# Where the rank product and the steps behind it stand among the shared expert's items

## The chip, the cores and the metric

One core of one Trainium2 chip. The time is the device time of one execution in microseconds; the median of three executions of the kernel before is 1052.46 us (1050.67 to 1053.14).

## What is computed

A residual stream `x` of 2 x 1024 tokens and 256 features passes four blocks, each behind a layer norm: attention with one key head, a feed-forward block, attention with ALiBi, and the same feed-forward block again. The change lies in the two feed-forward blocks:

```
shared_out = silu(x @ sw1.T) * (x @ sw2.T) @ sw3.T          # hidden 1024
scores = sigmoid(x @ router_w.T)                            # 8 experts
top_idx = top_k(scores + expert_bias, 2)
combine = the two scores, divided by their sum, at the two experts
h = silu(h1) * h2        # h1, h2 = x @ w12 of the expert, 128 wide
routed_out = sum over experts of (h @ w3) * combine
x = x + shared_out + routed_out
```

## The kernel before, in words

All engines run hand-written queues that meet at semaphores. Products that need fp32 accuracy are made of three passes over a high and a low part of each operand (lines 246 to 248 for an up product, line 1196 for a down product).

**Items.** The shared expert is cut into eight units of 128 hidden features and the tokens into four chunks of 512; `ITEMS` (line 45) orders the 32 pairs. Per item `e`, TensorE makes the up product `up(f, e)` (12 matmuls of 512 columns into banks 2(e mod 2) and 2(e mod 2)+1), ScalarE the gate `sg`, VectorE the product `hf` (`hidden`, L1893), ScalarE its high part `hh` (L1430), VectorE the low part `hl` (L1897), and TensorE the down product `down(f, e)`. TensorE's order is up(e), down(e-1), up(e+1), ... VectorE can't do anything between `hf` and `hl` of one item, since its queue is in order. Items 0 to 3 go before the loop that matters here (in `between`), items 4 to 15 in `feed_forward` ahead of the routed experts, 16 to 31 behind them. f is 0 or 1 for the two feed-forward blocks.

**Routing.** The tokens of each expert must be gathered into tiles before the routed products can start. That takes a long series of small VectorE steps, placed behind `hidden` of an item by two tables, `ROUTE_BEHIND` and `FIND_BEHIND` (item: stages), and by two TensorE products placed behind the up product of an item:

- `route` stages 0 to 2 (L1803 to L1819): the best two experts of each token, as a 0/1 table `chosen`.
- `count_ranks`, behind up(RANK_AT) (L1207, L1208): four matmuls over `chosen`, into `rank_bank`, which is the gate bank of the other parity than RANK_AT. It waits for `chosen` and for `hf` of the item before.
- `route` stage 3 (L1823, L1824): copies the ranks and counts out of that bank. It is called by item RANK_AT - 1, as the last of that item's work, and waits for the rank product. The up product of item RANK_AT + 1 waits for these copies.
- `route` stages 4 to 6 (L1827 to L1857): prefix sums and each token's place `pos`.
- `find` stages 0 to 6 (L1907 to L1928): from `pos` the tables `is_tile` (stage 1), four quarters of `in_tile` (stages 2, 3, 5, 6; L1921), `at_tile` (stage 4).
- `find_sources`, behind up(FIND_AT), FIND_AT = 13 (L1215): 32 matmuls over them. It waits for all of find 0 to 6.
- `find` stage 7 (L1933 to L1938), behind item 13: `source_f`, `source`. The up product of item 14 waits for `source_f` (L1935).
- POOL then issues the indirect DMAs that gather the rows (`fetch_rows`, L842), and TensorE turns them (`turn_rows`, L1231) ahead of and behind down(15).
- `route` stages 7 to 9: the two weights of each token and the experts' places, behind items 13 to 15.

**Weight splits.** Behind each odd item from 5 to 13 ScalarE casts (L1498) and VectorE subtracts (L1944) the weights of a further unit; `EXPERT_BEHIND` places the same two steps (L1504, L1950) for experts 6 and 7, and POOL splits the other six.

VectorE's order within an item (lines 1952 to 1964):

```
hidden(f, e)
for stage in FIND_BEHIND.get(e, ()):
    find(f, stage)
for stage in ROUTE_BEHIND.get(e, ()):
    route(f, stage)
if e in EXPERT_BEHIND:
    expert_low(f, EXPERT_BEHIND[e])
if e % 2 and RING <= (e + 3) // 2 < 2 * SHARED and e != 2 * SHARED - 1:
    unit_low(f, (e + 3) // 2)
if e == RANK_AT - 1:
    route(f, 3)
```

Of the kernel before, what the change touches and what calls it, by code (L numbers as in the profile page):

```python
# [44 lines left out]
ITEMS = [(u, 0) for u in range(3)] + [(u, 1) for u in range(3)] + [(u, c) for u in range(3, SHARED) for c in (0, 1)] + \  # L45
        [(u, c) for u in range(SHARED) for c in (2, 3)]
OPENING = 3
RANK_AT, FIND_AT = 6, 13
ROUTE_BEHIND = {3: (0,), 4: (1,), 5: (2,), 6: (4, 5), 7: (6,), 13: (7,), 14: (8,), 15: (9,)}
FIND_BEHIND = {8: (0, 1, 2), 9: (3,), 10: (4,), 11: (5,), 12: (6,), 13: (7,)}  # L50
FIND = 10
UNIT_IN_ROUTED = 4
EXPERT_BEHIND = {12: 6, 14: 7}
COMBINE_BEHIND = [{18: 3, 19: 3, 20: 3, 21: 1, 22: 3, 23: 3, 24: 1, 25: 1, 26: 1, 27: 3, 28: 3, 29: 3, 30: 3, 31: 1},
                  {**{e: 3 for e in range(18, 28)}, 28: 2}]
STATS_BEHIND = {21: 0, 24: 1}
# [195 lines left out]
def program(nc, x, w_a, b_a, fc_a, b_fc, w_b, fc_b, w_units, router, ebias, iota, consts, slopes, krows, out):  # L252
# [15 lines left out]
    with ExitStack() as ctx:  # L268
# [1052 lines left out]
        def _(act):  # L1321
# [104 lines left out]
            def high(f, e):  # L1426
                s = FS * f + e
                act.wait_ge(h_done, s + 1)
                wait(act, down_done, s - 1)
                act.copy(hh[:, e % 2, :], hf[:, e % 2, :]).then_inc(hh_done, 1)  # L1430
# [69 lines left out]
            def expert_high(f, e):  # L1500

                cols = slice(WIDTH * e, WIDTH * e + WIDTH)
                act.wait_ge(wexp_in[e], 16 * (f + 1))
                act.copy(wexp_h[:, cols], wexp_raw[:, cols]).then_inc(exp_high_done, 1)  # L1504

            def unit_item(f, e):

                gate(f, e)
                high(f, e)
                if e in EXPERT_BEHIND:  # L1510
                    expert_high(f, EXPERT_BEHIND[e])
                if e % 2 and RING <= (e + 3) // 2 < 2 * SHARED and e != 2 * SHARED - 1:
# [27 lines left out]
        def _(dve):  # L1540
# [345 lines left out]
            def hidden(f, e):  # L1886

                s = FS * f + e
                a = e % 2
                dve.wait_ge(silu_done, s + 1)  # L1890
                dve.wait_ge(u_ready, s + 1)
                wait(dve, hl_done, s - 1)
                dve.tensor_tensor(hf[:, a, :], bank[2 * a + 1], sg[:, a, :], ALU.mult).then_inc(h_done, 1)  # L1893
                if f == 0 and e in TURNED:
                    lows(2, TURNED[e])
                dve.wait_ge(hh_done, s + 1)
                dve.tensor_tensor(hl[:, a, :], hf[:, a, :], hh[:, a, :].bitcast(F32), ALU.subtract).then_inc(hl_done, 1)  # L1897
# [48 lines left out]
            def expert_low(f, e):  # L1946

                cols = slice(WIDTH * e, WIDTH * e + WIDTH)
                dve.wait_ge(exp_high_done, (NEXP - POOL_EXPERTS) * f + e - POOL_EXPERTS + 1)
                dve.tensor_tensor(wexp_l[:, cols], wexp_raw[:, cols], wexp_h[:, cols].bitcast(F32), ALU.subtract).then_inc(exp_low_done, 1)  # L1950

            def unit_item(f, e):
# [9 lines that stand above are left out]
# [177 lines left out]
```

## Time and profile before

| | |
|---|---|
| median of 3 executions | 1052.46 us (1050.67 to 1053.14) |
| the profiled execution's own time | 1053.91 us |
| its span, first to last instruction | 1052.2 us |
| mean granted TensorE clock | 0.988 |
| VectorE busy | 758.8 us (72%) |
| ScalarE busy | 589.2 us (56%) |
| GpSimd busy | 409.8 us (39%) |
| chain that ended last | PE 78%, DVE 13%, ACT 4%, issue 3%, POOL 2%, DMA 1% |

Engines: PE is TensorE's matmuls, PEld its weight loads, DVE VectorE, ACT ScalarE, POOL GpSimd, SP SyncE. Times in the timeline count from the start of the span. A row of the timeline is an instruction or a run of like ones: its start, how long it takes, engine, line, operation, what it writes and reads, and, in brackets, how long the engine had stood idle and who released it. Ends of matmuls are modelled, so the time that a product takes is best read from start to start. Items 4 to 15 of the first feed-forward block run from 346.69 to 401.12 us; in the second block they begin 518.79 us later.

### The profile page before, as it was taken

How to read it: one execution, taken by the hardware profiler on the slowest of the kernel's cores; microseconds unless marked ns; L12 is line 12 of the kernel's file. 1: busy time of each engine (PE TensorE's matmuls, PEld its weight loads, DVE VectorE, ACT ScalarE, POOL GpSimd, SP SyncE). 2: the span in 40 equal slices, each digit the busy share in tenths (PEclk: the TensorE clock that was granted, in tenths of full speed). 3: DMA queues.
4: the chain of work that ended last, by engine and by line, in shares of the span. 5: the costliest groups of instructions: out<-in, count | busy, mean ns of one | idle time of the engine just before them, and what ended most of it. 6: DMA issues, size and time to landing. Idle time of an engine off the chain costs nothing.

```text
span 1052.2 us, 19787 instructions
## 1 busy us (share of the span) xinstructions
PE 997.4 (95%) x6818; PEld 639.3 (61%) x6818; DVE 758.8 (72%) x1564; ACT 589.2 (56%) x1262; POOL 409.8 (39%) x434
## 2 busy tenths in 40 slices
PE   4789999999999999999989999999999999999998
PEld 3533433343348889988867433333443588899887
DVE  6788888888447686447778878888883658764575
ACT  4525776777764335653445657777777543466432
POOL 3420544322443507625743102322234362274470
PEclk9969999999999999999999999999999999999999
DMA  4721121110114315734249523244401151256351
GB/s 133 193 41 32 44 42 43 40 42 13 30 26 154 137 45 160 187 111 120 77 116 224 104 43 58 54 75 74 76 10 46 31 211 61 71 178 167 119 180 51
DMA packets 66756, 95.23 MB, mean 91 GB/s; under 512 B 19670, under 2 KB 50822, under 8 KB 64600
## 3 DMA queue, kind: packets, MB, share of 16 engines
q1 hardware_dynamic: 46645, 52.54, 18.3%
q10 hardware_dynamic: 13100, 22.53, 8.8%
q0 software_dynamic: 6912, 18.88, 7.0%
q8 instruction: 57, 0.93, 0.4%
q14 instruction: 42, 0.34, 0.1%
HBM read 66.59 MB, written 26.67 MB: 89 GB/s over the span
## 4 chain that ended last, share of the span: by engine, by line
PE 78%; DVE 13%; ACT 4%; issue 3%; POOL 2%; DMA 1%; ACTq 0%; SPq 0%; DVEq 0%; POOLq 0%
PE o_ps L1056 14%; PE st_ps L1038 11%; PE su_ps L997 8%; PE st_ps L246 7%; PE st_ps L247 7%; PE st_ps L248 7%; DVE mab L1678 5%; PE st_ps L997 4%; PE o_ps L1196 4%; PE su_ps L1196 3%; PE su_ps L1102 3%; ACT pt L1404 2%; PE st_ps L1231 2%; PE su_ps L1001 2%; PE su_ps L246 1%
## 5 line engine op out<-in xcount | busy, mean ns | idle before, releaser
L1404 ACT ACTIVATE pt<-st_ps 128x512 f32<-128x512 f32 (+3 forms) x768 | 329.0, 494 | 175.1 <-PE st_ps L1038 118.1
L1038 PE MATMUL st_ps<-qs,ks 99*128 99x512 bf16 (+9 forms) x768 | 245.2, 333 | 9.1 <-ACT pt L1404 6.2
L761 POOL TENSOR_SCALAR_AFFINE_SELECT pt<-pt 128x512 f32<-128x512 f32 x120 | 76.4, 637 | 352.0 <-ACT pt L1404 352.0
L1678 DVE TENSOR_REDUCE mab<-su_ps 128x1 f32<-128x512 f32 (+3 forms) x302 | 190.0, 659 | 22.9 <-PE su_ps L1001 16.4
L1056 PE MATMUL o_ps<-pt,vp 128*32 128x512 f32 (+3 forms) x1536 | 164.5, 503 | 1.9 <-POOL pt L761 1.0
L997 PE MATMUL su_ps<-ks,qs 102*128 102x512 bf16 (+7 forms) x538 | 160.8, 328 | 4.7 <-DVE mc L1678 2.7
L1038 PEld LDWEIGHTS st_ps<-qs,ks 99*128 99x128 bf16 (+2 forms) x768 | 73.7, 98 | 115.9 <-ACT pt L1404 64.4
L842 POOL DMA_INDIRECT rows_in<-rows,source x80 | 78.5, 981 | 98.0 <-DVE source L1938 73.7
L1678 DVE TENSOR_REDUCE mab<-st_ps 128x1 f32<-128x512 f32 (+2 forms) x152 | 100.2, 660 | 13.7 <-PE st_ps L1001 10.4
L1430 ACT CAST hh<-hf 128x512 fp32r<-128x512 f32 x64 | 39.7, 621 | 123.8 <-DVE hf L1893 123.8
L997 PEld LDWEIGHTS su_ps<-ks,qs 96*128 96x128 bf16 (+1 forms) x538 | 52.6, 98 | 83.1 <-DVE mab L1678 48.5
L246 PE MATMUL st_ps<-xt_h,wu 128*128 128x512 f32 x256 | 100.9, 394 | 1.4 <-DVE source_f L1935 0.9
L247 PE MATMUL st_ps<-xt_h,wu 128*128 128x512 f32 x256 | 100.3, 392 | 0.0
L248 PE MATMUL st_ps<-xt_l,wu 128*128 128x512 f32 x256 | 99.7, 389 | 0.0
L852 POOL DMA_INDIRECT back<-outs,pos x64 | 68.1, 1064 | 61.3 <-DMA outs<-rows_out 39.8
L997 PE MATMUL st_ps<-ks,qs 96*128 96x512 bf16 (+6 forms) x230 | 78.9, 356 | 4.9 <-DVE mc L1678 2.0
L1897 DVE TENSOR_TENSOR hl<-hf,hh 128x512 fp32r<-128x512 f32 x64 | 44.6, 696 | 42.6 <-ACT hh L1430 42.6
L1678 DVE TENSOR_REDUCE mc<-su_ps 128x1 f32<-128x512 f32 (+3 forms) x105 | 63.2, 620 | 15.7 <-PE su_ps L1001 15.7
L1001 PE MATMUL su_ps<-cstb 128*128 128x128 bf16 x370 | 70.9, 222 | 0.0
L1893 DVE TENSOR_TENSOR hf<-st_ps,sg 128x512 f32<-128x512 f32 x64 | 43.9, 686 | 29.1 <-PE st_ps L248 23.6
L1056 PEld LDWEIGHTS o_ps<-pt,vp 128*32 128x32 f32 x1536 | 31.1, 109 | 51.2 <-issue 35.9
L1423 ACT ACTIVATE sg<-st_ps 128x512 f32<-128x512 f32 x64 | 38.2, 597 | 42.8 <-PE st_ps L248 42.6
(230 smaller groups left out, 2033.3 us busy)
## 6 DMA issues: line engine op xcount, KB each, us to landing
wu_raw<-w_units_dram SPq DMA_DIRECT2D x32, 384.0 KB, 3.1
outs<-rows_out ACTq DMA_DIRECT2D x40, 256.0 KB, 2.8
q_parts<-hml SPq DMA_DIRECT2D x16, 384.0 KB, 3.3
wexp_raw<-w_units_dram SPq DMA_DIRECT2D x16, 384.0 KB, 7.1
inv<-inverses SPq DMA_DIRECT2D x128, 32.0 KB, 1.8
rows<-xn SPq DMA_DIRECT2D x8, 512.0 KB, 6.9
qs<-q_parts ACTq DMA_DIRECT2D x10, 384.0 KB
k_parts<-hml SPq DMA_DIRECT2D x8, 384.0 KB, 2.6
```

Source lines behind the costliest of these rows:

```text
L246: pe.matmul(out, lh, rh, start=n == 0, stop=False)
L247: pe.matmul(out, ll, rh, start=False, stop=False)
L248: last = pe.matmul(out, lh, rl, start=False, stop=n == len(terms) - 1)
L761: pool.affine_select(block, block, [[0, 4], [1, P]], ALU.is_ge, 0.0, base=0, channel_multiplier=-1).then_inc(masked, 1)
L842: pool.indirect_dma_start(rows_in[:, n % RPAIRS, a, :], None, rows, bass.IndirectOffsetOnAxis(ap=source[:, 2 * i + a:2 * i + a + 1], axis= ...
L997: last = pe.matmul(out_b[:, c0:c0 + width], query_columns(s, slice(0, rows), j0 + a, P * qt, P * qt + P), key_stack(l, s)(j0 + a)[0:rows, ...
L1001: last = pe.matmul(out_b[:, c0 + width - P:c0 + width], identb, mask_q, start=False, stop=True)
L1038: last = pe.matmul(bank[KM_BANKS[n % len(KM_BANKS)]][:, lo - CH * part:hi - CH * part], key_stack(l, s)(j)[0:rows, P * kt:P * kt + P], que ...
L1056: last = pe.matmul(o_ps[32 * j:32 * j + 32, lo:hi], vp[:, QT * b + kt, 4 * g + j if l else 4 * (g % 2), :], exponentials(s, q, lo, hi)[:, ...
L1196: last = pe.matmul(out_b, left, right, start=u == 0 and n == 0 and t % 2 == 0, stop=u == SHARED - 1 and n == 2, skip_group_check=True)
L1404: act.activation(exponentials(s, q, lo, hi)[:, j, :], bank[KM_BANKS[i % len(KM_BANKS)]][:, lo - CH * part:hi - CH * part], ACT.Exp, scale= ...
L1678: dve.tensor_reduce(to, bank[SU_BANKS[n % len(SU_BANKS)]][:, 0:share * width].rearrange("p (j k) -> p j k", j=share), AX.X, ALU.max).then_ ...
```

## The change

`RANK_AT` goes from 6 to 7, so the rank product goes behind item 7's up product, and the copies of its results behind item 6's `hidden` instead of item 5's. Route stages 4, 5 and 6 go behind items 7 and 8 (before: 6 and 7), find stages 0 to 6 behind items 9 to 12 (before: 8 to 12), and the split of expert 6 behind item 11 (before: 12), on ScalarE and VectorE. `rank_bank` changes with RANK_AT from bank 2 to bank 0.

```diff
-RANK_AT, FIND_AT = 6, 13
-ROUTE_BEHIND = {3: (0,), 4: (1,), 5: (2,), 6: (4, 5), 7: (6,), 13: (7,), 14: (8,), 15: (9,)}
-FIND_BEHIND = {8: (0, 1, 2), 9: (3,), 10: (4,), 11: (5,), 12: (6,), 13: (7,)}
+RANK_AT, FIND_AT = 7, 13
+ROUTE_BEHIND = {3: (0,), 4: (1,), 5: (2,), 7: (4,), 8: (5, 6), 13: (7,), 14: (8,), 15: (9,)}
+FIND_BEHIND = {9: (0, 1), 10: (2, 4), 11: (3,), 12: (5, 6), 13: (7,)}
 FIND = 10
 UNIT_IN_ROUTED = 4
-EXPERT_BEHIND = {12: 6, 14: 7}
+EXPERT_BEHIND = {11: 6, 14: 7}
```

## Rows read from the trace of the kernel before

**Rows 1.** The page, part 1: busy time of TensorE, weight loads and the others.

```profile
PE 997.4 (95%) x6818; PEld 639.3 (61%) x6818; DVE 758.8 (72%) x1564; ACT 589.2 (56%) x1262; POOL 409.8 (39%) x434
```

**Rows 2.** The waits of PE, 344 to 400 us: total, times, longest.

```profile
PE st_ps L1207 <- DVE chosen L1819: 0.7, 1, 0.7
PE st_ps L246 <- DVE source_f L1935: 0.5, 1, 0.5
PE su_ps L1196 <- DVE hl L1897: 0.3, 1, 0.3
```

**Rows 3.** The timeline of DVE, items 5 to 13 of the first feed-forward block.

```profile
357.57 0.69 DVE L1897 TENSOR_TENSOR hl<-hf,hh 128x512 fp32r<-128x512 f32 x1 [0.69 <-ACT hh L1430]
...
360.10 0.29 DVE L1823 COPY rank<-st_ps 128x128 f32<-128x128 f32 x1
...
360.50 0.68 DVE L1893 TENSOR_TENSOR hf<-st_ps,sg 128x512 f32<-128x512 f32 x1
...
362.48 0.42 DVE L1827 TENSOR_TENSOR_SCAN cum<-cst,filled 128x128 f32<-128x128 f32 x1
...
363.51 0.28 DVE L1837 TENSOR_REDUCE few<-over 128x8 f32<-128x128 f32 x1
...
388.10 1.22 DVE L1921 TENSOR_TENSOR in_tile<-steps_in,pos_partf 128x1024 bf16<-128x1024 f32 x1
389.24 0.95 DVE L1950 TENSOR_TENSOR wexp_l<-wexp_raw,wexp_h 128x768 fp32r<-128x768 f32 x1
390.11 0.68 DVE L1893 TENSOR_TENSOR hf<-st_ps,sg 128x512 f32<-128x512 f32 x1
...
392.31 0.20 DVE L1935 SCALAR_TENSOR_TENSOR source_f<-st_ps,source_f 128x40 f32<-128x40 f32 x1
392.55 0.18 DVE L1938 CAST source<-source_f 128x40 uint32<-128x40 f32 x1
```

**Rows 4.** The timeline of PE: first rows of products, items 5 to 14.

```profile
355.69 0.40 PE L246 MATMUL st_ps<-xt_h,wu 128*128 128x512 f32 x1
...
359.35 0.49 PE L1207 MATMUL st_ps<-chosen,cst 128*128 128x128 f32 x2 [0.75 <-DVE chosen L1819]
359.67 0.39 PE L1208 MATMUL st_ps<-chosen,cst 128*128 128x128 f32 x2
359.81 0.36 PE L1196 MATMUL su_ps<-wu,hh 128*128 128x256 f32 x1
...
361.33 0.40 PE L246 MATMUL st_ps<-xt_h,wu 128*128 128x512 f32 x1
...
364.08 0.28 PE L1196 MATMUL o_ps<-wu,hh 128*128 128x256 f32 x1
...
365.51 0.40 PE L246 MATMUL st_ps<-xt_h,wu 128*128 128x512 f32 x1
...
389.38 1.32 PE L1215 MATMUL st_ps<-at_tile,in_tile 128*128 128x80 bf16 x32
390.53 0.36 PE L1196 MATMUL o_ps<-wu,hh 128*128 128x256 f32 x1
...
392.66 0.47 PE L246 MATMUL st_ps<-xt_h,wu 128*128 128x512 f32 x1 [0.46 <-DVE source_f L1935]
```

**Rows 5.** The timeline of POOL: the first gather of the first block.

```profile
393.62 1.98 POOL L842 DMA_INDIRECT rows_in<-rows,source  x1 [36.91 <-DVE source L1938]
```

**Rows 6.** The timeline of ACT: expert 6's cast.

```profile
387.37 0.83 ACT L1504 CAST wexp_h<-wexp_raw 128x768 fp32r<-128x768 f32 x1
```

**Rows 7.** The timeline of PE: the second turn of gathered rows, first block.

```profile
403.06 0.66 PE L1231 MATMUL st_ps<-cst,rows_in 128*128 128x128 f32 x4 [1.34 <-DMA rows_in<-rows,source]
```

**Rows 8.** The timeline of PE: the first two turns of the second block.

```profile
919.90 1.03 PE L1231 MATMUL st_ps<-cst,rows_in 128*128 128x128 f32 x8
```

**Rows 9.** Windows: busy time of PE, PEld, DVE, ACT, POOL, granted clock, DMA share.

```profile
50.00:55.00 5.00, 3.62 (x15) 1.32 (x15) 4.90 (x11) 0.00 (x0) 0.00 (x0) 0.64 0.64 120
55.00:60.00 5.00, 4.73 (x17) 2.22 (x17) 4.09 (x8) 2.25 (x4) 0.00 (x0) 0.50 0.92 177
...
540.00:545.00 5.00, 3.15 (x14) 2.25 (x13) 5.00 (x11) 2.31 (x6) 2.87 (x3) 1.00 0.68 236
```

## The prediction

> **What bounds the kernel now.** I read the page first: TensorE (PE) is busy 95% of the span [rows 1], so a change of order can win only PE's waits, and can lose whatever new wait it makes. So the second view was PE's waits in the stretch that the change touches, items 3 to 15 of the first feed-forward layer. There are three, 1.5 us together [rows 2]: the rank product waits 0.7 us for `chosen`, item 14's up product 0.5 us for `source_f`, one down product 0.3 us for `hl`. The second layer repeats the first 518.79 us later, wait for wait.
>
> The third view was VectorE's (DVE) timeline [rows 3]. The reader is to see that every `hf` starts the moment the work in front of it ends: from 357.57 to 392.55 DVE waits for nothing but its own round trip through ScalarE (ACT) between `hf` and `hl`. Such a `hidden` costs DVE 1.98 us from `hf` to the next instruction (360.50 to 362.48) [rows 3]. The seven items 6 to 12 take it from 360.50 to 390.11, 4.23 us each. PE needs 2.75 us for an up product (361.33 to 364.08) and 1.43 for a down product (364.08 to 365.51) [rows 4], 4.18 per item. So PE is nominally the bound, but in this stretch DVE is as full as PE and runs behind it; it decides when `find_sources` can start: 389.38, 0.06 us behind the end of the last `in_tile` (388.10 + 1.22) [rows 3, 4].
>
> **The change part by part.** No instruction is added or removed; per layer the same work is reordered, and only the placing behind items differs. The queues of SP and POOL are as before: POOL's gathers wait for `source` alone [rows 5].
>
> Ranks behind item 7's up product. Removed: PE's wait. Item 6's up product starts at 355.69 and would end at 358.44; the rank product started at 359.35 [rows 4], so 0.91 us is gained here. `hl` of item 5 ends at 357.57 + 0.69 = 358.26 [rows 3], so item 5's down product can follow at 358.44. PE then: down 5 to 359.87, up 7 to 362.62, rank product there. Its results were out at 359.67 + 0.39 = 360.06, 0.71 behind its start, and PE was free for the next after 0.46 (359.35 to 359.81) [rows 4]. I take the same: results at 363.35, `rank` copied from 363.40.
>
> Where the wait goes: DVE. Now the copy of the ranks comes directly behind `hidden` of item 6 and the next instruction on DVE is queued behind it. Before, item 4's unit split (DVE L1944) filled the wait, and the copy started at 360.10 with no idle. After, `hf` of item 6 can start at 360.1 at the latest (360.50 less the 0.40 of the two copies) [rows 3], its `hidden` ends at 362.1, and DVE stands until 363.40. This is a wait that no row of before shows. Bounds: nothing, if the product were out when `hidden` ends; at most 2.75, a whole up product. I take 1.3, worked out above from rows on both sides.
>
> The stages behind items 7 to 12. The copies end at 363.80. What DVE did before from 362.48 (first instruction behind `hidden` 6) to 388.10 (the last `in_tile`) is 25.62 us, with no wait in it that another order would save. The new order has the same work there, and one thing more: expert 6's split now comes ahead of the last `in_tile` instead of behind it, 0.87 us (389.24 to 390.11) [rows 3]. So the last `in_tile` starts at 363.80 + 25.62 + 0.87 = 390.29 and ends at 391.51; `find_sources` starts at 391.57, **2.19 us later than before**. PE would be ready for it at about 388.7 (from 362.62: 0.46 for the ranks, six pairs of a down and an up product of 4.18 = 25.1, and 0.5 for a wait of item 11's down product for its `hl`, which DVE's lag by then makes), so it stands for 2.9 us in one piece. Cover check: DVE must not run out of input in between. `hf` of item 7 starts at 363.80, 1.0 us behind its product. Item 7 costs 1.98 + 1.03 (route stage 4, 362.48 to 363.51) + 0.87, so `hf` of item 8 starts at 367.68; its up product ends near 367.4. That margin of 0.3 is the thinnest. Items 8 to 11 then take (387.2 - 367.7) / 4 = 4.88 us each against PE's 4.18, so DVE only falls further behind.
>
> Bank of the ranks: item 8's up product now waits for the copies, at 363.9; it would start at 364.5. Nothing. Expert 6 on ACT: the 0.83 us cast [rows 6] now goes in front of item 12's gate, which is needed on DVE at 387.2; even with the unit cast of the same item it is done 1.4 us earlier. Nothing; without that cover at most 0.83.
>
> Behind find. Item 12's down product follows 1.15 us after `find_sources` starts (389.38 to 390.53), item 14's up product at 391.57 + 1.15 + 1.43 = 394.15, against 392.66 [rows 4]: 1.49 later, and the 0.5 us wait for `source_f` is gone (ready at 392.51 + 1.32 = 393.8). About 0.1 comes off, because that product no longer restarts a standing array. DVE: `hf` of item 13 moves from 390.11 to 391.43, 1.32 later, and with it `source`, POOL's first gather (393.62) [rows 5] and the landing. In the first layer PE waits 1.34 us for the gathered rows, to 403.06 [rows 7]: the landing decides, +1.32. In the second both first turns run together at 919.90 without a wait [rows 8]: PE decides, +1.4. The landings themselves are bounded: they may slip by less than 1.34 in the first layer where they meet other transfers; I take no slip. From there on PE, DVE and POOL are shifted alike, so nothing is given back.
>
> **Sum.** 1.32 + 1.4 = +2.7 us, of which the price of the rank wait is 1.3 per layer, expert 6's place 0.87 for find, less 0.9 that PE gained ahead and cannot spend. The profiled execution took 1053.91 us around a span of 1052.2, so 1056.6 for such a one; it stands 1.45 above the median of 1052.46, so the median becomes 1055.2.
>
> One term can be weighed against a rule. The rows show 0.46 us for the rank product with the array standing before it [rows 4]; that is what the sum uses. The Trainium skill (TensorE: Matmul & The Clock Gate, Architectural detail: the array is 16× 32×32, not 1× 128×128) says that TensorE can pull weight loads ahead of running matmuls; now that `chosen` is ready long before, the load would be hidden, an estimate of 0.1 us less per layer and +2.5 in place of +2.7. The wait row cannot show it.
>
> **The rivals.** About 0.2% (2.1 us) is what a measurement of this kernel can tell from no change.
> (a) My forecast, 0.67: 1055.2, between 1.5 and 3.8 us above before.
> (b) The ranks come while `hidden` 6 still runs, so DVE does not stand. Then only the 0.87 us of expert 6 delays find, and DVE reaches `source` when it did: 1052.5. For it: PE is 1.46 us ahead at item 7 (359.87 for 361.33). Against: the product must be out before 362.1, and item 7's up product alone ends at 362.62. 0.15, mostly for a DVE stretch that has slack I don't see.
> (c) Faster: PE's order decides to the end of the stage. The wait for `chosen` goes (0.91), and find waits no longer than before: 1.0 us per layer, 1050.5. It decides if the last `in_tile` ends before 388.2 (362.62 + 0.46 + 25.1), so DVE would have to be 3.3 us quicker over items 6 to 12 than I work out. Nothing shows that. 0.08.
> (d) TensorE's clock falls in the new 2.9 us hole. The rows show a granted clock of 0.64 and then 0.50 (half speed, 1.2 GHz) over 50 to 60 us, behind a sparsely used PE; that stretch lost 5 x 0.36 + 5 x 0.50 = 4.3 us of full speed. Against it, 540 to 545 stands idle for 1.85 of 5 us and keeps 1.00 [rows 9]. Once in one layer: 1055.2 + 4.3 = 1059.5. 0.10. The Trainium skill (the same page, What's actually happening) has TensorE at half rate after it stood idle for long enough and at full rate after sustained work; by it the length of the hole decides, and the trace agrees in so far as the hole of 540 to 545 cost nothing, while no row of this case has one of 2.9 us between dense products.
>
> **How the numbers follow.** The predicted time is (a)'s. The range 1051.4 to 1058.2 leaves out (c) and (d), and takes in (b) and the bounds of the rank wait and the landings for (a). Of (a)'s 0.67 some 0.13 lies under the 0.2% bound. Faster 0.08; same 0.15 + 0.13 = 0.28; slower 0.54 + 0.10 = 0.64.
>
> **What the changed profile would show.** Right: no wait of PE for `chosen`; DVE idle 1.3 us before `rank`, released by PE; item 11's down product waiting some 0.5 us for `hl`; PE idle nearly 3 us before L1215, released by `in_tile`; no wait for `source_f`; `source` 1.3 us later in both layers, and the turns of gathered rows as much. Wrong: a `rank` copy with no idle before it (b), a find wait under 0.5 us (c), or a granted clock under 1.00 within 390 to 400 us (d). If DVE has idle time before `hf` of item 8, the thin margin was no margin and the loss is larger.

## The result, and the profile after

| | before | changed |
|---|---|---|
| median of 7 executions | 1053.47 us | 1058.99 us |
| lowest and highest | 1050.67, 1054.10 | 1054.54, 1061.12 |
| profiled execution, own time and span | 1053.91, 1052.2 | 1054.54, 1052.8 |
| mean granted TensorE clock | 0.988 | 0.990 |

The ratio is 1.0046, 95% interval 1.0031 to 1.0061: the change makes the kernel slower by 4.8 us (3.3 to 6.4; the two medians lie 5.5 apart). I had forecast slower by 2.7 and a range up to 1058.2, so the direction was right and the size too small; the median of 1058.99 lies 0.8 above the range. One microsecond of that distance is no fault of the change's account: the median before is 1053.47 over seven executions, and I had started from 1052.46, that of three.

The profiled execution is the fastest of the seven and ends only 0.6 us behind that of before. So spans don't compare the two; places inside the stage do. The copy of the scores (L1784) opens it, and the time from there to a later instruction of the stage, up to the first turn of gathered rows, repeats mostly to 0.01 to 0.05 us between traces of one kernel, where the clock does not fall (0.10 in e11 and e15). Behind that turn it does not: it scatters by microseconds. Up to that copy the changed kernel's execution was 2.98 us ahead (343.81 for 346.79), by chance of the first attention: in fifteen further traces, whose code is the same up to there, the copy lies anywhere between 344.09 and 350.14. Behind it the changed kernel loses 2.17 us by the second block's copy and 1.41 in the second block: 0.6 = -2.98 + 2.17 + 1.41.

The waits of PE in the changed kernel, 344 to 402 us (total, times, longest), against [rows 2]:

```profile
PE st_ps L1215 <- DVE in_tile L1921: 2.7, 1, 2.7
PE su_ps L1196 <- DVE hl L1897: 0.6, 2, 0.3
```

The waits for `chosen` and `source_f` are gone; one wait of the find product stands in their place, nearly twice as long as the three of before together. The timeline of DVE, to be read against [rows 3]:

```profile
357.03 0.68 DVE L1893 TENSOR_TENSOR hf<-st_ps,sg 128x512 f32<-128x512 f32 x1
...
360.29 0.29 DVE L1823 COPY rank<-st_ps 128x128 f32<-128x128 f32 x1 [1.20 <-PE st_ps L1208]
...
386.16 2.35 DVE L1921 TENSOR_TENSOR in_tile<-steps_in,pos_partf 128x1024 bf16<-128x1024 f32 x2
388.43 0.68 DVE L1893 TENSOR_TENSOR hf<-st_ps,sg 128x512 f32<-128x512 f32 x1
...
390.86 0.18 DVE L1938 CAST source<-source_f 128x40 uint32<-128x40 f32 x1
```

DVE stands 1.20 us for the ranks, where it stood for nothing before. The timeline of PE in the first block, against [rows 4]:

```profile
359.65 0.38 PE L1207 MATMUL st_ps<-chosen,cst 128*128 128x128 f32 x2
...
388.56 1.37 PE L1215 MATMUL st_ps<-at_tile,in_tile 128*128 128x80 bf16 x32 [2.68 <-DVE in_tile L1921]
389.74 0.56 PE L1196 MATMUL o_ps<-wu,hh 128*128 128x256 f32 x1
...
392.44 0.63 PE L246 MATMUL st_ps<-xt_h,wu 128*128 128x512 f32 x1
```

Item 12's down product takes 2.70 us from start to start (389.74 to 392.44) where a down product takes 1.43. The windows say why; the column before the last two is the granted clock:

```profile
388.00:389.00 1.00, 0.43 (x12) 0.44 (x13) 1.00 (x2) 0.00 (x0) 0.00 (x0) 1.00 0.00 0
389.00:390.00 1.00, 1.00 (x26) 1.00 (x23) 0.32 (x2) 0.86 (x2) 0.00 (x0) 0.85 0.00 0
390.00:391.00 1.00, 1.00 (x6) 1.00 (x7) 0.93 (x5) 0.49 (x1) 0.00 (x0) 0.50 0.00 0
...
392.00:393.00 1.00, 1.00 (x6) 0.90 (x5) 0.82 (x1) 0.00 (x0) 1.00 (x1) 0.50 0.00 0
393.00:394.00 1.00, 1.00 (x6) 0.83 (x5) 0.00 (x0) 0.00 (x0) 0.92 (x1) 0.95 0.00 0
```

Some 1.1 us after the hole's end the clock falls, and TensorE works at half clock (1.2 GHz) for some 3 us. The second block has the same hole and no such stretch; its up product of item 14 follows the find product by 2.65 us, where the first block's took 3.88:

```profile
909.53 1.32 PE L1215 MATMUL st_ps<-at_tile,in_tile 128*128 128x80 bf16 x32 [2.68 <-DVE in_tile L1921]
...
912.18 0.40 PE L246 MATMUL st_ps<-xt_h,wu 128*128 128x512 f32 x1
```

### The profile page after: what moved, and what is told of

Read it like the earlier page. It is cut to its first block, busy times and chain, and to the rows that moved or that the text cites. A ratio compares the mean times of both kernels' runs of the same rounds, so it can differ in the third digit from the quotient of the medians.

```text
span 1052.8 us, 19785 instructions
## 1 busy us (share of the span) xinstructions
PE 994.1 (94%) x6818; PEld 637.6 (61%) x6818; DVE 758.9 (72%) x1564; ACT 588.7 (56%) x1262; POOL 411.3 (39%) x434
## 4 chain that ended last, share of the span: by engine, by line
PE 76%; DVE 14%; ACT 4%; issue 3%; POOL 2%; DMA 1%; ACTq 0%; SPq 0%; DVEq 0%; POOLq 0%
PE o_ps L1056 14%; PE st_ps L1038 11%; PE su_ps L997 7%; PE st_ps L246 7%; PE st_ps L247 7%; PE st_ps L248 7%; DVE mab L1678 5%; PE o_ps L1196 4%; PE su_ps L1196 4%; PE st_ps L997 4%; PE su_ps L1102 2%; ACT pt L1404 2%; PE st_ps L1231 2%; PE su_ps L1001 2%; PE su_ps L246 1%
## 5 line engine op out<-in xcount | busy, mean ns | idle before, releaser
L246 PE MATMUL st_ps<-xt_h,wu 128*128 128x512 f32 x256 | 100.9, 394 | 0.4 <-DVE xt_l L1570 0.4
```

Of the source, the lines that this page charges most:

```text
L246: pe.matmul(out, lh, rh, start=n == 0, stop=False)
```

## The experiments

All comparisons inside the stage are in one measure: microseconds from the copy of the scores, less the same in the kernel before, first block / second block. Positive is later; the values are good to 0.02 us.

| kernel | find product starts | `source` | up product of item 14 | first turn of gathered rows |
|---|---|---|---|---|
| forecast for the change | 2.19 | 1.32 | 1.49 | - |
| changed kernel | 2.16 / 2.17 | 1.29 / 1.29 | 2.76 / 1.54 | 2.97 / 1.46 |
| e1, the same | 2.17 / 2.16 | 1.81 / 1.29 | 3.70 / 3.08 | 4.27 / 3.00 |
| e9, the same | 2.20 / 2.20 | 1.86 / 1.34 | 3.02 / 1.59 | 2.93 / 1.51 |
| e2, hole filled | 2.18 / 2.16 | 1.30 / 1.29 | 1.56 / 1.54 | 1.47 / 1.45 |
| e3, unit 4 in the rank wait | 2.15 / 2.17 | 1.79 / 1.30 | 2.92 / 1.56 | 2.82 / 1.47 |
| e5, expert 6 behind find | 1.30 / 1.29 | 1.30 / 1.28 | 1.30 / 1.28 | 1.28 / 1.27 |
| e6, before with expert 6 behind 11 | 1.09 / 0.86 | 0.22 / -0.01 | 0.47 / 0.25 | 0.37 / 0.16 |
| e7, expert 6 in the rank wait | 1.29 / 1.31 | 0.42 / 0.43 | 0.68 / 0.69 | 0.58 / 0.60 |
| e8, splits on GpSimd | 4.29 / 4.54 | 3.42 / 3.66 | 3.67 / 3.93 | 3.57 / 3.83 |
| e11, before with late splits | -0.23 / -0.24 | -0.69 / -0.70 | -0.70 / -0.71 | -0.69 / -0.70 |
| e12, and scores from PSUM | -1.42 / -1.41 | -1.88 / -1.87 | -1.89 / -1.88 | -1.90 / -1.86 |

The experiments ran in five groups. In that of e5 to e8 the kernel before takes 1054.67 us, like in the result; in the other four it takes 1087.7 to 1092.9 us, and single executions of it lie up to 15 us apart. I call these the slower groups; what makes them slower was not found. It need not be the chip: e5 to e8 and the slower e13 to e16 are on record under the same chip number. The table's measure is the same in both kinds: before's own second trace (e4) agrees with its first to 0.01 us in every column. The whole times of the slower groups are weak evidence.

**The changed kernel again (e1), and with TensorE kept at work in the hole (e2).** My theory of the surplus: the hole lets the clock fall. The rival: it comes from the opening.

> The changed kernel once more, for a second trace. Clock theory (the new hole of 2.7 us in front of the find matmuls lets the granted clock fall to 0.50 behind it in some executions, in one block or both): find_sources starts 2.2 us and item 13's hf 1.3 us later than before relative to the start of the stage, in both blocks; the stretch behind the hole is at 0.50 for some 3 us in one or both blocks, and the time is 3 to 7 us above before. Rival (the surplus over my 2.7 us arises elsewhere, in the first attention's opening, whose clock is low in stretches): the holes look as in the first trace, and the span up to the copy of the scores (L1784) is longer than the 346.8 us of before by the surplus.

> The changed kernel with 15 idle bf16 matmuls of 384 columns (results unused) in front of the wait of find_sources, so that TensorE works through the hole while VectorE's order and every start of the find matmuls stay. Clock theory: no stretch under 1.00 behind the find matmuls, and the time falls by 1.5 to 3.5 us against the changed kernel, to 2 to 3.5 us above before. Rival (elsewhere): the time stays within 1 us of the changed kernel, about 5 us above before.

```diff
 def find_sources(f):
-    pe.wait_ge(find_step, FIND * f + FIND - 1)
     pe.wait_ge(h_done, FS * f + FIND_AT)
+    for _ in range(15):
+        pe.matmul(found_bank[:, P:4 * P], identb, cstb[:, :, :].rearrange("p a m -> p (a m)"), start=True, stop=True)
+    pe.wait_ge(find_step, FIND * f + FIND - 1)
```

e1: in both blocks the clock fell, item 14 came 3.70 and 3.08 us late. The windows of 8 us behind each find product of e1:

```profile
390.40:398.40 8.00, 8.00 (x55) 7.36 (x56) 3.56 (x10) 1.95 (x3) 3.50 (x3) 0.61 0.08 22
931.74:939.74 8.00, 8.00 (x65) 7.49 (x66) 4.17 (x11) 2.01 (x4) 3.83 (x4) 0.79 0.15 44
```

And of e2, where the find product starts at the same place of the stage (0.22 us of hole left, the rest filled):

```profile
394.91 1.32 PE L1217 MATMUL st_ps<-at_tile,in_tile 128*128 128x80 bf16 x32 [0.22 <-DVE in_tile L1923]
```

```profile
394.91:402.91 8.00, 8.00 (x73) 7.30 (x74) 5.11 (x13) 3.31 (x5) 3.87 (x3) 1.00 0.12 35
935.08:943.08 8.00, 8.00 (x73) 7.29 (x74) 5.12 (x13) 3.31 (x5) 3.84 (x4) 1.00 0.17 49
```

VectorE's lateness is untouched (find 2.18 later, source 1.30), and item 14 comes 1.56 and 1.54 later, what I had forecast (1.49). One pair could be chance, since the clock doesn't fall behind every hole; with the three more pairs below (no fall behind 8 filled holes, 7 behind 12 unfilled ones) it is shown inside the stage that the idle array is what lets the clock fall. The whole times don't show it: e1 1.0016 (0.9997 to 1.0036), e2 1.0026 (1.0010 to 1.0042).

**e4, the kernel before again.**

> The kernel before once more, for a second trace of it. Both theories: every wait of the feed-forward stage as in the first trace (0.7, 0.5 and 0.3 us). The rival expects the stretch up to the copy of the scores to differ from 346.8 us by some us, as it does between the two first traces (343.8 in the changed kernel's).

Its copy of the scores lies at 346.33; every column of the table is as in the first trace. It is the reference trace for the slower groups.

**Unit 4's split in the wait for the ranks (e3).**

> The changed kernel with unit 4's low part (L1944, 0.87 us) moved from behind item 5 to behind item 6, ahead of the copies of the ranks, so that it lies in VectorE's wait for the ranks. My theory (VectorE's queue decides when find starts): the wait in front of the rank copy falls from 1.2 to about 0.3 us, find starts 0.9 us earlier, the hole falls from 2.7 to 1.8 us, and the time falls by 1.7 us, and by the clock's share as well (together 2 to 4). Rival (TensorE's order decides, VectorE's wait is free): time unchanged within 0.5 us.

```diff
-if e % 2 and RING <= (e + 3) // 2 < ...:
+if e % 2 and e != 5 and RING <= (e + 3) // 2 < ...:
     unit_low(f, (e + 3) // 2)
+if e == 6:
+    unit_low(f, 4)
 if e == RANK_AT - 1:
     route(f, 3)
```

A miss, and a useful one. The wait stayed as it was:

```profile
361.13 0.95 DVE L1944 TENSOR_TENSOR wu<-wu_raw,wu 128x768 fp32r<-128x768 f32 x1
363.28 0.29 DVE L1823 COPY rank<-st_ps 128x128 f32<-128x128 f32 x1 [1.20 <-PE st_ps L1208]
```

Item 6's `hf` comes 0.88 us earlier for it and the split follows; the copy waits for a rank product whose time TensorE sets. Work that already lay ahead of the wait shortens nothing when it is moved into it. Only what lay behind it does, which is e7. Ratio 1.0023 (1.0008 to 1.0039).

**Which part of the change costs what (e5, e6, e7).** e5 takes expert 6 out of the way of find, e6 is the expert's move alone, e7 fills the rank wait with it.

> The changed kernel with the split of expert 6 back behind item 12, so behind the last in_tile; ranks and stages stay as changed. My theory (the find matmuls start when VectorE's queue, pinned by the end of the rank product, has done its work): in both blocks find starts 1.29 us later than before relative to the copy of the scores, in place of 2.16; source stays 1.29 later; item 14's up product now waits again for source_f and comes 1.3 later (1.54 in the changed kernel without a fall of the clock); the hole is 1.8 to 1.9 us. Clock theory: with a hole under 2 us the clock stays at 1.00. Time 2 to 3 us above before, below the changed kernel by 2. Rival (the place of expert 6 is free, only the ranks' place counts): find still 2.16 later.

> The kernel before with only the split of expert 6 moved from behind item 12 to behind item 11; ranks behind item 6 as before. My theory: find starts 0.87 us later than before, source not later, item 14's up product 0.1 to 0.2 later, hole in front of find 1.1 us, no fall of the clock: time within 0.5 us of before. Rival (expert 6's place is what costs): item 14's up product 0.9 us or more later in both blocks, 2 us in the time.

> The changed kernel with expert 6's split moved to behind item 6, into VectorE's wait for the ranks. Unlike unit 4's split, which lay in front of the wait already, this takes 0.87 us out of the work behind the ranks. My theory: the wait before the rank copy falls from 1.2 to 0.35 us, find 1.29 and source 0.42 us later than before (in place of 2.16 and 1.29), item 14's up product 0.5 to 0.6 later, no fall of the clock; time 1 us above before. Rival (VectorE's wait is not what delays source): source still 1.29 later.

```diff
# e5, from the changed kernel
-EXPERT_BEHIND = {11: 6, 14: 7}
+EXPERT_BEHIND = {12: 6, 14: 7}
# e6, from the kernel before
-EXPERT_BEHIND = {12: 6, 14: 7}
+EXPERT_BEHIND = {11: 6, 14: 7}
# e7, from the changed kernel
-EXPERT_BEHIND = {11: 6, 14: 7}
+EXPERT_BEHIND = {6: 6, 14: 7}
```

The waits of PE in e5 around find, from the timeline:

```profile
387.98 1.32 PE L1215 MATMUL st_ps<-at_tile,in_tile 128*128 128x80 bf16 x32 [1.82 <-DVE in_tile L1921]
...
391.26 0.47 PE L246 MATMUL st_ps<-xt_h,wu 128*128 128x512 f32 x1 [0.45 <-DVE source_f L1935]
```

Find came 1.30 later, 0.87 less than in the changed kernel, and item 14 waits for `source_f` again, 1.30 and 1.28 late: expected 1.29 and 1.3. Time 1.0028 (1.0010 to 1.0046), 2.9 us, as expected. So the ranks' place alone, with the stages behind it, costs 1.3 us per block and carries the larger part of the loss. e6: find 0.86 later in the second block, source on time, item 14 0.25 later (expected 0.1 to 0.2); in the first block item 4's `hf`, ahead of the edit, was already 0.21 late. Time 1.0008 (0.9993 to 1.0023). The expert's move alone costs little, because find was hidden from `source` by `hf` of item 13.

In e7 the wait for the ranks shrank from 1.20 to 0.22:

```profile
362.89 0.29 DVE L1823 COPY rank<-st_ps 128x128 f32<-128x128 f32 x1 [0.22 <-PE st_ps L1208]
```

Find 1.29 and 1.31 later, source 0.42 and 0.43 (expected 1.29 and 0.42), item 14 0.68 (expected 0.5 to 0.6). Time 0.9996 (0.9982 to 1.0010): 0.87 us of split work, put into the wait instead of behind it, takes 0.87 us off the lateness of item 14, and the whole time is again within the measurement of before (-1.9 to 1.1 us), although item 14 still comes 0.68 late. In e5 and e7 the hole before find is 1.8 us and the clock kept 1.00 in all four; four are too few to call such a hole safe, as a hole of 1.85 us elsewhere shows (the section on why the prediction was partly right).

**VectorE relieved by GpSimd (e8).** If VectorE's queue is the bound, taking four splits of 0.87 us (3.5 us) out of it ahead of find should make the changed order pay.

> The changed order, with VectorE relieved: experts 6 and 7 wholly, and the low parts of units 5, 6 and 7, on GpSimd, which stands idle from 356 to 393 us. My theory (VectorE's queue is the bound of this stretch, and the moved rank product pays only where it isn't): find starts 0.6 to 0.7 us earlier than before and item 14's up product 1.3 to 1.5 earlier in each block, source 1.5 earlier, no hole, no fall of the clock; time 2.5 to 3 us below before. Rival (GpSimd's work slows VectorE or comes late for the up products): new waits of PE for wu or slower instructions on VectorE, and no gain.

```diff
-POOL_EXPERTS = 6
+POOL_EXPERTS = 8
+POOL_UNITS = (5, 6, 7)
-EXPERT_BEHIND = {11: 6, 14: 7}
+EXPERT_BEHIND = {}
# ... behind split_expert on GpSimd; VectorE leaves these units out, and two waits are
# fitted to the new owner of the splits (not shown)
+for n in POOL_UNITS:
+    _, r = unit_turn(f, n)
+    pool.wait_ge(unit_high_done, LATE * f + n - RING + 1)
+    pool.wait_ge(unit_low_done, LATE * f + n - RING)
+    pool.tensor_tensor(wu[:, r, 1, :], wu_raw[:, r, 1, :], wu[:, r, 0, :].bitcast(F32), ALU.subtract).then_inc(unit_low_done, 1)
```

The rival won: 1.0068 (1.0047 to 1.0089), 7.2 us slower, item 14 3.67 and 3.93 later. VectorE's timeline of e8:

```profile
360.10 1.90 DVE L1824 TENSOR_TENSOR chosen<-eq,eq 128x128 f32<-128x128 f32 x1
...
367.68 1.58 DVE L1836 TENSOR_TENSOR over<-few,steps_in 128x128 f32<-128x128 f32 x1
```

and GpSimd's:

```profile
359.80 1.97 POOL L832 TENSOR_TENSOR wexp_l<-wexp_raw,wexp_h 128x768 fp32r<-128x768 f32 x1
367.23 1.89 POOL L869 TENSOR_TENSOR wu<-wu_raw,wu 128x768 fp32r<-128x768 f32 x1 [5.46 <-ACT wu L1503]
```

`chosen` took 0.37 us before and takes 1.90, ending at 362.00, 0.23 behind GpSimd's subtraction (361.77); `over` took 0.29 and takes 1.58, ending at 369.26 behind one that ends at 369.12. Two more instructions ahead of `chosen` suffer: the cast `idf` (L1819, at 357.15) takes 1.84 instead of 0.17, and the first `eq` (at 359.02) 0.84 instead of 0.29. An instruction that reads PSUM kept its length while GpSimd subtracted (`hf` at 355.18: 0.67, GpSimd's from 353.84 to 355.68). Item 6's `hf` came 3.24 us late, and the rank product stood 1.8 us for it. That GpSimd shares its SBUF interfaces with VectorE, and that VectorE instructions with two SBUF inputs contend for them, is what the Trainium skill states (GPSIMD Engine Reference, Specifications); the rows of `chosen` and `over` agree, and add the size: the small instruction lasts to just behind the end of the large one.

**Less work on VectorE ahead of `source` (e11, e12).** The same clash is in the kernel before, with nothing changed: the first instruction of route stage 0, and what GpSimd does then:

```profile
348.99 1.93 DVE L1803 TENSOR_TENSOR sel<-sc,ebb 128x128 f32<-128x128 f32 x1
```

```profile
348.60 2.17 POOL L831 TENSOR_TENSOR wexp_l<-wexp_raw,wexp_h 128x768 fp32r<-128x768 f32 x1
```

> The kernel before (ranks behind item 6) with VectorE's work ahead of source cut by 0.87 us and ahead of find by 0.87 as well: the split of expert 6 behind item 13, where VectorE has idle time, the low part of unit 7 behind item 12. My theory: find 0.2 us earlier (TensorE's order is then the bound), source 0.87 earlier, item 14's up product 0.8 to 0.9 earlier in each block; time 1.6 us below before. Rival (source_f is not what holds item 14): 0.2 earlier and no more.

> The same, and the addition of the expert bias to the scores reads them from PSUM, before their copy, instead of from SBUF. In the kernel before that instruction (L1803, 128x128) takes 1.93 us where like ones take 0.29; with more splits on GpSimd three further VectorE instructions with two SBUF inputs took 0.84 to 1.90 us, each to the end of GpSimd's subtraction. Theory (such a VectorE instruction stands while GpSimd runs one with two SBUF inputs): the addition takes 0.3 us, VectorE is 1.6 us ahead from item 4 on, PE waits neither for hl of item 3 nor for chosen, find 1.4 to 1.7 us and item 14's up product 1.9 to 2.3 us earlier than before in each block (relative to the copy of the scores); time 4 us below before. Rival (the instruction is slow by itself, by its broadcast input): still 1.9 us, and the time as in the run without it.

```diff
# e11, from the kernel before
-EXPERT_BEHIND = {12: 6, 14: 7}
+EXPERT_BEHIND = {13: 6, 14: 7}
-if e % 2 and RING <= (e + 3) // 2 < ...:
+if e % 2 and e != 11 and RING <= (e + 3) // 2 < ...:
     unit_low(f, (e + 3) // 2)
+if e == 12:
+    unit_low(f, 7)
# e12 adds, in between(), ahead of the copy of the scores (a wait for the bias moves with it)
+dve.tensor_tensor(sel[:, :, :], bank[6][:, 0:TT * NEXP].rearrange("p (t e) -> p t e", e=NEXP),
+                  ebb[:, :].unsqueeze(1).to_broadcast([P, TT, NEXP]), ALU.add).then_inc(rt_step, 1)
# and in route, stage 0
-dve.tensor_tensor(sel[:, :, :], sc[:, :, :], each(ebb[:, :]), ALU.add).then_inc(rt_step, 1)
```

e11: find 0.23 earlier (expected 0.2), item 14 0.70 (expected 0.8 to 0.9). e12: the addition takes 0.29 us when it reads PSUM:

```profile
348.70 0.29 DVE L1786 TENSOR_TENSOR sel<-su_ps,ebb 128x128 f32<-128x128 f32 x1 [5.81 <-PE su_ps L1120]
...
357.70 1.49 DVE L1899 TENSOR_TENSOR hl<-hf,hh 128x512 fp32r<-128x512 f32 x1 [0.69 <-ACT hh L1430]
```

```profile
347.84 1.82 POOL L831 TENSOR_TENSOR wexp_l<-wexp_raw,wexp_h 128x768 fp32r<-128x768 f32 x1
...
356.79 1.85 POOL L831 TENSOR_TENSOR wexp_l<-wexp_raw,wexp_h 128x768 fp32r<-128x768 f32 x1
```

It does so while GpSimd subtracts (347.84 to 349.66), and with the same broadcast input, so the rival that the instruction is slow by itself is refuted.

VectorE is 2.0 us ahead at item 5, find 1.42 and item 14 1.89 us earlier in both blocks (expected 1.4 to 1.7 and 1.9 to 2.3); `chosen` is still waited for, 0.3 us in place of 0.7. The lead of 2.0 us shrinks to 1.2 there, because the clash comes back in another place: item 5's `hl` (357.70) meets GpSimd's next subtraction and takes 1.49 us, where it took 0.69; e16 and the second blocks show the same. In the whole time e11 has 0.9983 (0.9964 to 1.0002) and e12 0.9989 (0.9970 to 1.0008). Both ran again:

> The kernel before with expert 6's split behind item 13 and unit 7's low part behind item 12, again: item 14's up product 0.70 earlier in each block as in its first trace, time 1.2 to 1.8 us below before.

> The same with the scores' addition reading PSUM, again: item 14's up product 1.9 earlier in each block as in its first trace; time 3 to 4 us below before where nothing behind the stage gives it back.

e15: 0.9987 (0.9964 to 1.0011), item 14 0.61 / 0.70 earlier. e16: 0.9976 (0.9951 to 1.0001), 1.88 / 1.90 earlier. All four lean to faster than before, and each interval still touches no change; the gain inside the stage is shown, that of the whole kernel is likely and not established.

**Filled against unfilled, three more pairs.**

> The changed kernel a third time, beside the same kernel with the hole filled. By the traces so far (two of the changed kernel and one with unit 4 in the rank wait, six holes of 2.7 us): find 2.16 and source 1.29 us later in each block; item 14's up product 1.54 later where the clock keeps 1.00 and 2.8 to 4.3 later where it falls, which it should in one block or both. Time 3 to 6 us above before.

> The changed kernel with TensorE kept working through the hole, again. Clock theory: item 14's up product 1.54 us later in both blocks, no stretch under 1.00 behind find, time 2 to 3.5 us above before and below the changed kernel of the same call by 1 to 3. Rival (the falls of the clock cost nothing that lasts): same time as the changed kernel.

> The changed kernel, beside the filled one. Clock theory: a fall in the first block's hole (four of four so far), in the second's in some executions (one of four); time 4 to 6 us above before. Rival (the falls' cost does not last): 2.7 us, as the filled one.

> The changed kernel with the hole filled by idle matmuls. Clock theory: no fall, item 14's up product 1.55 later in both blocks, time 2 to 3.3 us above before and 1.5 to 3 below the changed kernel. Rival: the same time as the changed kernel.

> The changed kernel. Clock theory: the first block's hole lets the clock fall (five of five so far), the second's seldom (one of five); on a chip where before takes about 1053 us, 4 to 6 us above before. On a slower chip 2 to 5.

> The changed kernel with the hole filled. Clock theory: no fall, item 14's up product 1.55 us later in both blocks; on a chip where before takes about 1053 us, 2.3 to 3.3 us above before, 1.5 to 2.5 below the changed kernel. Rival (the fall does not last into the time): the same as the changed kernel.

| pair | unfilled: first turn late, ratio | filled: first turn late, ratio |
|---|---|---|
| e1, e2 | 4.27 / 3.00, 1.0016 (0.9997 to 1.0036) | 1.47 / 1.45, 1.0026 (1.0010 to 1.0042) |
| e9, e10 | 2.93 / 1.51, 1.0037 (1.0017 to 1.0057) | 1.49 / 1.50, 1.0027 (1.0006 to 1.0047) |
| e13, e14 | 3.02 / 1.46, 1.0019 (0.9998 to 1.0041) | 1.44 / 1.46, 1.0024 (1.0006 to 1.0042) |
| e17, e18 | 1.45 / 2.85, 1.0017 (0.9996 to 1.0038) | 1.46 / 1.45, 0.9992 (0.9965 to 1.0020) |

With the result's trace and e3 there are six executions with the 2.7 us holes. The clock fell in 7 of the 12 holes, at least once in every execution; in the eight filled holes it never fell. My guess that it is always the first block's was refuted by e17. What a fall costs at the first turn of gathered rows is what stands above 1.47: 1.50 in the result's trace, 2.80 and 1.53 in e1, 1.35 in e3, 1.46, 1.55 and 1.38 in e9, e13, e17; together 11.6 us in six executions, 1.9 each. The mean ratio of the four unfilled runs is 1.0022, of the filled 1.0017. In microseconds the unfilled kernel is 0.6 us slower than the filled one over the four pairs: -0.5 to 1.6 by the scatter of the single executions, -1.4 to 2.5 by that of the four pairs. So in the slower groups the 1.9 us at the first turn is not found again in the whole time; the numbers lean against its lasting in full and don't exclude it. The unfilled kernel is 2.5 us above before there (1.6 to 3.5 by single executions), not 4.8.

## Why the prediction was partly right

**The bound.** Right: VectorE's queue, pinned at one end by the rank product, sets when find and `source` come. The forecast chain had the rank wait at 1.3 us (measured 1.20), find 2.19 later (2.16 and 2.17), `source` 1.32 (1.29 in both), item 14's up product 1.49 (1.54 where the clock held), PE's hole 2.9 (2.68), no wait for `source_f`. e5 and e7 move find and `source` separately, by the 0.87 us and to the values computed. The term I added for item 11's down product was two waits of 0.3 us instead of one of 0.5. The price of the ranks' place, 1.3 us per block, is shown by e5, where expert 6 stands as before: 1.30 and 1.29 at find, and 2.9 us in the whole time (1.1 to 4.9).

**The landing.** In the first block I took the wait for gathered rows as staying 1.34 us [rows 7], so +1.32. In the result's trace that wait is gone, since TensorE, slowed by the clock, came later than the rows; item 15's down product is 1.68 later. The landing thus absorbed 1.3 us of the first turn's 2.97; what is left of the clock's 1.50 there is 0.36 above my 1.32. The landing itself is less fixed than I took it: the second turn comes 0.52 later in e4, which is the kernel before, 1.60 in e5 and 0.34 to 0.59 in the four filled kernels.

**The weight load.** I had weighed one term against the Trainium skill (TensorE: Matmul & The Clock Gate, Architectural detail: the array is 16× 32×32, not 1× 128×128), which says that TensorE can pull a weight load ahead of running matmuls. The trace agrees, with the 0.1 us that I estimated: the load starts at 359.42, with the last matmul of the up product, and the rank product takes 0.36 us from start to start (359.65 to 360.01) in place of 0.46. The wait was 1.20 instead of 1.3.

```profile
359.42 0.41 PEld L1207 LDWEIGHTS st_ps<-chosen,cst 128*128 128x128 f32 x2
```

**What failed: the clock behind the new hole, put at nothing in the sum.** I gave it a chance of 0.10, as rival (d), once in one block, at 4.3 us. It falls behind 7 of the 12 new holes and in every execution at least once, and costs 1.4 to 2.8 us each at the first turn of gathered rows, 1.9 per execution.

The evidence I set against it was the row of 540 to 545 [rows 9]. Its hole is one of 1.85 us (before L246 at 544.32), and I carried it over to one half as long again. It does not even hold for its own length. The same instruction stands behind the same hole in all 20 traces, and in 7 of them (e4, e5, e6, e8, e10, e12, e16) the clock falls behind it, as in e5:

```profile
543.22 0.58 PE L246 MATMUL st_ps<-xt_h,wp_h 128*128 128x512 f32 x1 [1.85 <-DVE yr L1584]
```

```profile
543.22:548.22 5.00, 5.00 (x23) 4.32 (x24) 2.89 (x11) 2.35 (x5) 3.29 (x4) 0.66 0.70 151
```

The row that I read was one of the 13 that escaped. One execution with the full clock says little about a hole that sometimes lets it fall.

How much of the 4.8 us this explains is open. Adding the term to the sum gives 2.7 + 1.9 = 4.6 us, but that agreement is partly luck, since the 1.9 is read ahead of the landing, which absorbs most of a fall in the first block (above). Between the two profiled executions the changed kernel loses 3.58 us behind the copy of the scores (2.17 + 1.41), 0.9 above my 2.7. Its four repetitions in the slower groups have falls too and lie 2.5 us above before. No filled kernel ran where before takes 1053 us. So the clock term was wrongly left out, the place and the frequency of the falls are shown, and the rest of the distance between 2.7 and 4.8 has no shown cause.

**Faster or the same.** (b) and (c) are refuted: the rank copy has its idle time, find its wait. The Trainium skill's rule on the clock (TensorE: Matmul & The Clock Gate, What's actually happening) stood on the right side, in that TensorE does fall to half rate after standing idle. My reading of it, that the length of the hole decides, is not borne out: holes of one length fell in 7 of 12 and in 7 of 20 cases.

## What to carry to other kernels

When two engines are equally full over a stretch, moving a product later on one can cost the other a wait that the first cannot give back; ask what the waiting engine could do behind its wait, and put that in front of it (e7). Work already ahead of a wait gains nothing by being moved into it (e3). A new idle stretch of TensorE among dense products should be priced with what the clock does behind it, and a similar hole at full clock in one trace does not clear it: look at the same hole in several executions. A loss that is read ahead of a wait for data is not yet a loss behind it.

## What the runs showed of the hardware

- A hole of 2.68 us between dense products is followed, in 7 of 12 cases, by about 3 us or more at a granted clock of 0.50; one of 1.85 us in another place (before L246 at 544.32 in the kernel before) in 7 of 20; the holes of 1.8 us before find in e5 and e7 in none of 4. The span of 2.68 filled with idle bf16 matmuls is followed by none in 8. Why a given hole escapes was not found.
- A small VectorE instruction with two SBUF inputs that starts while GpSimd's 128x768 subtraction runs lasts until 0.14 to 0.23 us behind its end: 1.93 us for 0.29 (before), 1.90 for 0.37 and 1.58 for 0.29 (e8). A 128x512 one took 1.49 for 0.69 and ended 0.55 behind (e12), a cast with one input 1.84 for 0.17 (e8). Reading one operand from PSUM restores 0.29. Putting further weight splits on GpSimd cost 7.2 us here (5.0 to 9.4).
- The same program took about 1053 us in some groups of runs and 1088 to 1093 in others, with one group of each kind under the same chip number; the cause was not found. From the first turn of gathered rows to item 16's `hf` it needed 63.8 us in the first trace of before (401.12 to 464.89) and 74.6 in e4 (400.65 to 475.29); the stage ahead of it was equal to 0.01 us.
